# A cross-attention that takes its batches in pairs, and a router that writes the expert picks before the destinations

## The reference, cut to what matters

```python
def cross_attn(x, context, Wq, Wk, Wv):          # x: 16 x 64 x 512, context: 16 x 1601 x 512
    Q = x @ Wq
    K, V = (context @ Wk, context @ Wv)
    energy = jnp.einsum('bqd,bkd->bqk', Q, K)
    lengths = jnp.sum(energy[:, 0] != 0, axis=-1)
    pad = kidx[None, None, :] >= lengths[:, None, None]
    energy = jnp.where(pad, NEG_INF, energy)
    score = jax.nn.softmax(energy / np.sqrt(DK), axis=-1)
    return jnp.einsum('bqk,bkd->bqd', score, V)
...
x = x + xattn(layernorm(x), ctx)     # self-attention, cross-attention, two-layer network, each with a norm
x = x + recurrent(layernorm(x))      # convolution, gates, linear recurrence
x = x + experts(layernorm(x))        # 8 experts, top 2, at most 160 rows for each of an expert's two choices
```

## Time and profile before

| | |
|---|---|
| median of 3 runs | 1009.5 us (1008.39 to 1009.78) |
| the profiled execution, its own time | 1006.8 us |
| its span, first to last instruction | 1005.1 us |
| TensorE busy | 985.9 us, 98% |
| VectorE, ScalarE, GpSimd busy | 61%, 39%, 21% |
| TensorE in the chain that ended last | 85% |
| DMA in that chain | 6%, of it 3% `in_ctxT` and 2% `in_ctx` |
| DMA over the span | 206.91 MB |

### The profile page before, as it was taken

How to read it: one execution, slowest core, us unless ns; L and a number is a source line. 1 busy time by engine, 2 the same in 40 slices (tenths; PEclk the granted TensorE clock), 3 DMA queues, 4 the chain that set the end, 5 groups by cost and what they waited for, 6 DMA issues and landing times.

```text
span 1005.1 us, 14411 instructions
## 1 busy us (share of the span) xinstructions
PE 985.9 (98%) x5412; PEld 777.0 (77%) x5412; DVE 614.8 (61%) x1142; ACT 393.7 (39%) x631; POOL 215.9 (21%) x202
## 2 busy tenths in 40 slices
PE   7999999999999999999999999899999999999998
PEld 4886444445454468878888887899999999999997
DVE  6368443344655565896466668577665666656666
ACT  3332211222111143355667542444544444445441
POOL 2053400002000036454422124720000000000051
PEclk9999999999999999999999999999999999999999
DMA  9809599999999922033311100885764756645543
GB/s 295 317 1 381 241 361 417 409 414 397 415 396 408 388 94 74 1 92 108 110 42 38 32 1 7 277 283 156 217 188 151 206 159 196 189 155 183 152 150 133
DMA packets 45959, 206.91 MB, mean 206 GB/s; under 512 B 5760, under 2 KB 16256, under 8 KB 41680
## 3 DMA queue, kind: packets, MB, share of 16 engines
q1 hardware_dynamic: 40256, 187.95, 52.6%
q0 software_dynamic: 5648, 18.22, 5.4%
HBM read 190.04 MB, written 16.12 MB: 205 GB/s over the span
## 4 chain that ended last, share of the span: by engine, by line
PE 85%; DVE 7%; DMA 6%; issue 1%; ACT 0%; SPq 0%; POOL 0%; DVEq 0%; ACTq 0%
PE ps L486 59%; PE ps L621 7%; PE ps L650 7%; DMA big<-in_ctxT 3%; DMA big<-in_ctx 2%; DVE stats L1315 2%; PE ps L480 2%; PE ps L598 1%; PE ps L951 1%; PE ps L856 1%; PE ps L978 1%; PE ps L654 1%; PE ps L631 1%; PE ps L493 1%; DVE hr L1324 1%; PE ps L532 1%
## 5 line engine op out<-in xcount | busy, mean ns | idle before, releaser
L486 PE MATMUL ps<-x,w 128*128 128x320 f32 x1536 | 235.6, 309 | 0.0
L486 PEld LDWEIGHTS ps<-x,w 128*128 128x128 f32 x1536 | 228.0, 188 | 0.4
L1839 DVE TENSOR_TENSOR w<-big,w 128x1536 fp32r<-128x1536 f32 x64 | 112.1, 1753 | 78.3 <-ACT w L1249 78.3
L486 PE MATMUL ps<-hsplit,w 128*128 128x320 f32 x672 | 107.7, 309 | 0.0
L1249 ACT CAST w<-big 128x1536 fp32r<-128x1536 f32 x64 | 94.2, 1475 | 29.2 <-PE ps L486 27.0
L486 PEld LDWEIGHTS ps<-hsplit,w 128*128 128x128 f32 x672 | 100.8, 188 | 0.1
L486 PE MATMUL ps<-xcT,u 128*128 128x512 f32 x432 | 98.2, 389 | 0.0
L621 PE MATMUL ps<-big 128*64 128x512 f32 (+2 forms) x512 | 95.9, 500 | 0.7 <-DVE s_stat L1495 0.6
L486 PEld LDWEIGHTS ps<-xcT,u 128*128 128x128 f32 x432 | 81.0, 188 | 17.0 <-DVE xcT L1627 0.2
L650 PE MATMUL ps<-big 128*64 128x512 f32 x384 | 86.4, 597 | 1.7 <-DMA big<-in_ctx 1.5
L621 PEld LDWEIGHTS ps<-big 128*64 128x64 f32 x512 | 44.2, 136 | 51.0 <-issue 39.1
(11 more groups left out here) (336 smaller groups left out, 1544.6 us busy)
## 6 DMA issues: line engine op xcount, KB each, us to landing
big<-in_ctxT SPq DMA_DIRECT2D x16, 3202.0 KB, 19.3
big<-in_ctx SPq DMA_DIRECT2D x16, 3072.0 KB
big<-in_w_units SPq DMA_DIRECT2D x64, 768.0 KB, 4.4
big<-in_dense_units SPq DMA_DIRECT2D x41, 256.0 KB, 2.7
xs<-big POOLq DMA_DIRECT2D x1, 5120.0 KB, 17.4
big<-in_gate_units SPq DMA_DIRECT2D x12, 384.0 KB, 3.0
hr<-xs SPq DMA_DIRECT2D x28, 160.0 KB, 5.8
ys<-big POOLq DMA_DIRECT2D x28, 160.0 KB, 5.6
```

The costliest lines, as they stand in the source:

```text
L486: mm = nc.tensor.matmul(dst, lhs[x], rhs[w], start=start and x + w == 0, stop=stop and x == 1)
L1839: V.tensor_tensor(wsplit[f % RING][1][:], wraw[f % RING], wsplit[f % RING][0][:].bitcast(F32), ALU.subtract).then_inc(w_low, 1)
```

## The change

**Cross-attention.** The loop has nine steps, one for a pair of batches and one more. One half of the columns has the first batch of the pair and the other half the second, each with all 1601 keys. The exchange between the halves, `output_sum`, the two-part softmax and the clearing of the pad are gone; VectorE's and ScalarE's instructions on the scores go over 1601 columns instead of 833, half as often. The scores fill four banks. Columns and rows come in pieces of a quarter of 2048 (512 keys, four of the twelve key tiles, so three pieces): one piece is 1 MB for each of the two batches, and columns and rows go through one ring of five places. The 65 keys left over have loads of their own. A load waits until TensorE has used the piece five before it (`piece_used`). The order is columns 0, columns 1, rows 0, columns 2, rows 1, and so on. The late queries are computed whole, one chunk in each of steps 0 to 3; `value_rows` runs in steps 5 to 8, a tile ahead of `values` and a tile behind it, in step 8 only the one behind. The decay series is taken two terms a step.

**Router.** VectorE computes the place in the pick matrix (`rt` row 1) by one addition, writes the picks for tiles 0 to 3, 4 to 5 and 6 to 7 from it, and computes the destinations after them. TensorE's order around it is changed: `first_expert_rows` runs in parts (0,4), (4,6), (6,8), `ranks_within(1)` stands before `first_expert_rows(3, 0)`, and ScalarE copies the last transposed tile before it rounds the last tile's rows.

```diff
+PAIRS = B // 2
+PIECES = KT // 4
+RINGS = 5
...
-VALUE = {9: 0, 10: 1, 11: 2, 12: 3, 13: 4, 14: 5, 16: 6}
+VALUE = {5: (0, 1), 6: (2, 3), 7: (4, 5), 8: (None, 6)}
...
+            def load_pieces(rows, p):
+                for piece in range(PIECES):
+                    g = loads[0]
+                    loads[0] += 1
+                    if g == 2:
+                        for i in range(NT):
+                            wait_filled(sp, "z", i)
+                    if g >= RINGS:
+                        sp.wait_ge(piece_used, g - RINGS + 1)
+                    for half in range(2):
+                        n, to = 2 * p + half, context_at[g % RINGS][half]
+                        if rows:
+                            keys = a["ctx"][n, 0:KT * P, :].rearrange("(p k) d -> p k d", k=KT)
+                            load(to, keys[:, 4 * piece:4 * piece + 4, :], context_in[g % RINGS])
+                        else:
+                            load(to, a["ctxT"][n * PIECES + piece].rearrange("p (c k) -> p c k", c=DC), context_in[g % RINGS])
...
             load_columns(0)
+            for p in range(1, PAIRS):
+                load_columns(p)
+                if p == 5:
+                    sp.wait_ge(late_q, DC)
+                    for k in range(DC):
+                        load(z2_raw[k], a["dense_units"][k], u_in[k])
+                load_rows_of(p - 1)
+            load_rows_of(PAIRS - 1)
+            sp.wait_ge(piece_used, 2 * PAIRS * PIECES - PIECES)
...
+            def scores(p):
...
+                for piece in range(PIECES + 1):
+                    if piece < PIECES:
+                        g = used[0]
+                        used[0] += 1
+                        pe.wait_ge(context_in[g % RINGS], 32 * (g // RINGS + 1))
...
+                    for d in range(DC):
+                        for half in range(2):
+                            n, w = 2 * p + half, 512 if piece < PIECES else TAIL
+                            mm = nc.tensor.matmul(ps[half * S:half * S + S, 2 + piece, 0:w], qT[:, d, n * S:(n + 1) * S],
+                                                  columns_in[half][:, d, :], start=(d == 0), stop=(d == DC - 1))
+                    mm.then_inc(piece_used if piece < PIECES else e_done, 1)
...
+            for p in range(PAIRS + 1):
+                if p < PAIRS:
+                    scores(p)
+                if p == 0:
+                    late_transposes(4, NT - 1)
+                    tail_and_count(0)
+                    late_transposes(NT - 1, NT)
+                    late_queries(0)
+                    continue
+                transpose_probabilities(p - 1)
+                if p >= 2:
+                    transpose_output(p - 2)
+                tail_and_count(p)
+                if p < PAIRS // 2:
+                    late_queries(p)
+                ahead, behind = VALUE.get(p, (None, None))
+                if ahead is not None:
+                    value_rows(ahead, 3 * p)
+                values(p - 1)
+                if behind is not None:
+                    value_rows(behind, 3 * p)
...
             split_transposes("t2", 0)
             split_transposes("t2", 1)
-            transpose_output(B - 1)
+            transpose_output(PAIRS - 1)
             split_transposes("t2", 2)
-            pe.wait_ge(o_evac, 2 * B - 1)
+            pe.wait_ge(o_evac, PAIRS)
             split_transposes("t2", 3)
-            value_rows(NT - 1)
+            value_rows(NT - 1, 3 * PAIRS)
...
+            for p in range(PAIRS + 1):                       # VectorE
+                if p < PAIRS:
+                    count_keys(p)
+                tail_and_count(p)
+                if p < PAIRS:
+                    shift(p)
+                if p:
+                    normaliser(p - 1)
+                if p >= 2:
+                    output_low(p - 2)
+                for i in VALUE.get(p, ()):
+                    if i is not None:
+                        second_norm(i)
...
+                if p == 8:
+                    decay_end()
+            output_low(PAIRS - 1)
...
+            first_expert_rows(0, 0)
             logits(1, 5, 4, 6)
-            first_expert_rows(0, 0)
             transposed_tiles(6, 7)
-            ranks_before()
-            logits(1, 6, 4, 6)
             first_expert_rows(1, 0)
             transposed_tiles(7, 8)
+            logits(1, 6, 4, 6)
+            logits(2, 7, 7, 7)
             first_expert_rows(2, 0)
-            logits(2, 7, 7, 7)
+            ranks_before()
+            ranks_within(1)
             first_expert_rows(3, 0)
-            ranks_within(1)
-            for d in range(DC):
-                first_expert_rows(d, 1)
+            for q in (1, 2):
+                for d in range(DC):
+                    first_expert_rows(d, q)
...
             last_transposed(6)
+            last_transposed(7)
             rows_high(7)
-            last_transposed(7)
...
             one_hot(1)
             positions(1)
-            pick_rows(1)
+            pick_rows(4, 6)
+            pick_rows(6, 8)
+            destinations(1)
```

More of the change, by code:

```diff
@@ L610, in scores @@
+            used = [0]
+            def scores(p):
+                if p:
+                    pe.wait_ge(shifted, p)
+                else:
                     for c in range(DC - 1):
                         wait_evacuated(pe, "q", c)
-                for piece, (lo, *widths) in enumerate(PIECES):
-                    if piece and n % 2 == 0:
-                        pe.wait_ge(pad_cleared, n // 2 + 1)
+                if p == PAIRS // 2:
+                    pe.wait_ge(late_q_out, DC)
+                for piece in range(PIECES + 1):
[3 more added lines that the diff above has]
+                        pe.wait_ge(context_in[g % RINGS], 32 * (g // RINGS + 1))
+                        columns_in = context_at[g % RINGS]
+                    else:
+                        pe.wait_ge(column_tail_in[p % 2], 16 * (p // 2 + 1))
+                        columns_in = column_tails[p % 2]
@@ L615, in scores @@
                     for d in range(DC):
-                        if n == 0 and d == DC - 1:
+                        if p == 0 and piece == 0 and d == DC - 1:
                             wait_evacuated(pe, "q", DC - 1)
-                        for half in (WIDE[n], 1 - WIDE[n]):
-                            narrow = half != WIDE[n]
-                            col, w = narrow * KA + lo, widths[narrow]
+                        for half in range(2):
+                            n, w = 2 * p + half, 512 if piece < PIECES else TAIL
@@ L846, in ranks_before, with first_expert_rows @@
                                      start=(i == 0), stop=False)
[L848 to L851 removed]
+            def first_expert_rows(d, q):
+                pe.wait_ge(picked, q + 1)
+                if q == 0:
                     wait_bank_free(pe, "gx", d)
[L853 removed]
+                for i in range(*((0, 4), (4, 6), (6, 8))[q]):
                     pe.wait_ge(row_low, i + 1)
@@ L1134, in _ @@
                     nc.scalar.copy(fbias[:], lnw[:, 6, :]).then_inc(fb_high, 1)
+                if p == 4:
+                    for u in range(DC):
+                        unit_high(u)
             def transposed_high(name, i):
@@ L1569, in _ @@
                     V.tensor_tensor(fbias[S:P, :], lnw[S:P, 6, :], fbias[S:P, :].bitcast(F32), ALU.subtract).then_inc(fb_low, 1)
-            output_sum(B - 1)
-            output_low(B - 1)
+                if p == 3:
+                    decay_start()
+                if 4 <= p < 8:
+                    for k in range(ATANH_TERMS - 2 - 2 * (p - 4), max(ATANH_TERMS - 4 - 2 * (p - 4), 0), -1):
+                        decay_term(k)
+                if p == 8:
+                    decay_end()
+            output_low(PAIRS - 1)
             dve.wait_ge(lnw_in, 16)
@@ L1782, in _ @@
             dve.wait_ge(slots_in, 16)
-            pick_rows(0)
+            pick_rows(0, 4)
+            destinations(0)
             last_norm(7)
```

456 lines of the change are left out of this document (177 added, 279 removed).

## The result

Four runs of the changed kernel have a median of 1016.19 us (1014.86 to 1016.67), four of the kernel before 1009.0 (1008.39 to 1009.78): a ratio of 1.0069, interval 1.0053 to 1.0085. A second set gave 1014.9 us and 1.0063 (1.0044 to 1.0083). The forecast was 1007.5, with a range that ended at 1013.

A forecast was written before the change was run, and what follows sets the result against it. TensorE and DMA limits overlap in the cross-attention loop; after the change DMA sets its end. Loop with its end 1.4 us slower, router 3.2 faster: 1009.5 - 1.8 = 1007.7, forecast 1007.5 us, 8-in-10 range 1002 to 1013.

The forecast's parts named there:

- TensorE's part of a pair: Cross-attention loop: 24.7 us of TensorE work per pair, against 26.8 for two old steps; TensorE alone would finish about 346.
- E: End of the last values in the cross-attention loop; forecast at 358.5 us, against 364.4 before the change.
- The DMA's part: Cross-attention loop: 95.2 MB from 118 us at 406 GB/s, last piece landing at 354.3; DMA, not TensorE, sets the end.
- rival 2: Pieces from pair 3 on move slower: 396 GB/s costs 4.2 us, giving 1011.7 (0.42 us per GB/s); chance 0.14.
- The signs that I had set: Prediction wrong if later-loop DMA share is under 0.95, rate outside 398 to 414 GB/s, or tail short passes over 2 us a pair.
- The tail: Behind the last values: VectorE's work on tile 6 delays tile 7 of `value_rows`; `fc1_half` starts at E + 13.3, before E + 6.0.
- The half clock: TensorE idles before tile 7 of `value_rows`, so its clock is halved for 3.4 us, costing 1.7 us.
- The router's gain: Routing: less TensorE idling and no clock fall, 4.3 us, plus 0.3 from moving the logits up: 4.6 us faster.
- its loss: First expert: the second expert's rows land later, VectorE stands 2.6 us, TensorE waits 1.4; router nets 3.2 us faster.
- The base: Whole kernel: profiled execution of 1006.8 us, with the median of the runs 2.7 above it, 1009.5, as starting point.
- Rivals 3 and 4: Loop: 3, ring too shallow, 48 us, 1055, chance 0.03; 4, clock falls in waits for pieces, 1012.6, chance 0.08.
- rival 4: Loop: TensorE's clock falls while waiting for pieces; each fall costs 1.7 us, making a piece 6.8 us; three give 1012.6; chance 0.08.

The follow-up runs named there:

- e1: Only the new routing, picks and order of the last copies, put into the kernel before with its old loop: 1003.65 us, ratio 0.9941 to the kernel before.

## Why the prediction was wrong, step by step

**TensorE's part of a pair was right**, its sum over the loop 4 us short. Forecast 24.7 us. The chain has 159.42 and 187.50 as the starts of two pairs' scores, 28.08 with a chunk of late queries at 3.67: 24.4. Taking 18.0 us of waits out of E gives 350, against 346. The step of before was misread on the way: the pieces of the earlier trace rows add up to 15.8 us, not 16.2, so two steps without extra work are 26.0 us and the pair saves less than I had.

**The DMA's part failed first.** The forecast let 95.2 MB run from 118 to 353 at 406 GB/s and the last piece land at 354.3. The first load was issued at 116.50 as worked out (forecast 116.0), and the last piece came at 363.54: 388 GB/s over all, 398 in the full part. E was 368.05, not 358.5: 9.5 us. An estimate from the rates above splits it: at 350 us the queue was 1.8 MB behind the forecast, 4.4 us at 406 GB/s; the 3.6 MB left then took 13.5 us, 4.6 more than at 406. The runs show the reason: with the row tails on 128 partitions E is 359.5, and there 417 GB/s carry 2.1 MB more than I had counted. I had put the risk on the rows of 8 KB (rival 2), and had given the sixteen small loads no price beyond their bytes, without a reason. Rival 2 has the right sign, but its mechanism is not what happened: with undisturbed rows of 8 KB the rate is 417, over the 406 I used. Nor does its price fit: 0.42 us for each GB/s is too little for 95.2 MB (235 us / 406 is 0.58), and no mean rate of the full part has the slow end in it. Nor did 406 mean a full queue: I wrote that pieces can't pass a full share by much since 1.01 already gives 406. The same loop of before moves 425 GB/s at a share of 1.00 with padded tails. So the earlier trace rows already had the holes in them, and I took a depressed rate for a limit: a packet of 25616 bytes of the columns takes 1031 ns on average in the kernel before from 152 to 340 us, 958 with padded tails. The signs that I had set couldn't show it either, since the share stayed at 1.0 and the rate on the edge of 398.

**The tail was mis-sized by 2.55 us.** Forecast E + 13.3, measured 15.85. The order of events was right down to `output_low`. Too small were `second_norm(6)`, 5.9 us and not 4.0 because of the two stretched gain instructions, and `decay_end`, 1.6 and not 0.8, its first instruction 1.22 us. That made `output_low` 2.8 us later than forecast. The half clock came as forecast (0.73 granted from 372 to 379, 0.77 from 380.5 to 384, so part of it at 1.2 GHz), and cost a little less: from the end of TensorE's wait to fc1 4.52 us, against 3.28 in the run with both queues reordered, 1.2 us and not 1.7. The forecast also saw only VectorE. The second queue, GpSimd, which held the `fc1` units behind tile 6's root, showed only when VectorE had been mended. Reordering both took 6.8 of the 9.8 us that the tail had grown by; the other 3.0 are tile 6.

**The router's gain was right, its loss wasn't.** Forecast 4.6 less in the routing and 1.4 given back; 4.7 with nothing given back (e1's 636.0 against 640.7 behind E), in the changed kernel, with the longer tail taken out, 3.7 in the first profile and 4.7 in the second. The loss was to come from the second expert's rows: VectorE was to stand 2 to 3 us for them. It stood 0.9 us in the first profile and not at all in the second, so these rows had more slack than by my sum.

**The base was 2.7 us too high.** I added to the sum the distance between the first profile (1006.8) and the median (1009.5). The second profile, 3.1 us later in E and 3.2 in time, shows that this distance is E's own scatter. I conclude that it doesn't carry over to a loop whose E is forecast by itself; the changed kernel's first profile was 0.3 us over its median. That E fell out early in the one profile I worked from was bad luck, adding it was the error. The terms make up the miss of 8.7: +9.5 for E, +2.55 for the tail, -2.7 for the base, -0.5 for the router, 8.9.

**Rivals 3 and 4.** The ring was deep enough to keep the share at 1.0 up to 356 us. The clock did fall after a wait for a piece (2.33 us, with 0.77 granted from 240 to 244), and made the 16 matmuls behind it 5.27 us long in place of 3.65, as rival 4 priced it. But TensorE still waited 0.35 us for the piece after that, so it cost nothing behind it.

**What stays open** is why only 128 partitions leave the pieces alone. The Trainium skill ("SBUF — State Buffer", section "Door 1: The DMA port swizzle (why `[64,N]` ≈ `[32,N]`)") states that partitions 0 to 63 reach only eight of the sixteen ports, and all 128 reach sixteen. By that rule tails of 64 partitions crowd half of the ports, and those of 65 nearly so, which fits. By the same section's table 96 partitions reach all sixteen, though eight of them with half as many partitions as the other eight, and here 96 partitions gave 271 GB/s where 128 gave 424. So the number of ports alone doesn't explain it; an uneven load on them would fit all four. That, and shares of the engines that aren't those of the pieces, go together in these runs: the traces don't say which engine moved a packet, so nothing here tells the two apart.

## What to carry to other kernels

A DMA share of 1.0 is no proof of a full rate: cut the stretch into pieces of 4 us and look for holes before taking its mean for a limit, and try small loads that lie among big ones on all 128 partitions. When two limits lie on top of each other, relieving the one buys nothing; here the cheaper limit to move was the other, and it made the old loop as good as the new. When work is reordered behind a phase, list every in-order queue that it passes, for the first mend only shows the next queue.

## What the hardware showed that I had not expected

- Row tails of 64, 65 and 96 partitions among loads of 128 cut the rate once a pair, for 4 to 8 us, at a DMA share of 1.0; the lowest slice of 4 us has 220 to 350 GB/s at each place. The same rows padded to 128 don't (424 GB/s from 240 to 244). Padding took 8 us off, net of some 5 us that the zeros cost by their bytes (2.1 MB at about 400 GB/s).
- VectorE's gain instructions, with two operands in SBUF, took 1.75 and 1.63 us beside GpSimd's, and 0.75 without (`L1353` and `L1357` from 373.57 and from 356.08 in the changed kernel). The Trainium skill ("SBUF — State Buffer", section "Who interferes with whom") says that the two engines share a port pair by an exclusive lock. The trace agrees that they hold each other up, with 1.0 and 0.9 us added on VectorE; whether by a lock, no run here shows. Even a chained instruction on 6 columns took 1.22 us (`L1470`), where `L1466`, a like one with GpSimd idle, took 0.16.
- With a load queue that is never empty the clock of TensorE still fell once in the changed kernel's loop, after a wait of 2.33 us: 0.77 granted from 240 to 244 us.
